# Two PSUM accumulators, deeper rings and bounded row gathers in the edge-gather stage of a GAT + MoE kernel

## What is computed

```python
xp = (x @ W).reshape(N, H, C)                       # N = 3125, H = 4, C = 256
e = leaky_relu(a_src[src] + a_dst[dst], 0.2)        # edges and self loops
ee = jnp.exp(e - m[dst])                            # m: segment max
msgs = xp[src] * (ee / z[dst])[:, :, None]
out = jax.ops.segment_sum(msgs, dst, num_segments=N)   # the stage that is changed
```

## Time and profile before

| | us |
|---|---:|
| median of 3 runs (2448.95 to 2456.05) | 2454.21 |
| the profiled execution | 2455.99 |
| its span, first to last instruction | 2454.2 |

### The profile page before, as it was taken

How to read it: one execution, slowest core, us unless ns; L and a number is a source line. 1 busy time by engine, 2 the same in 40 slices (tenths; PEclk the granted TensorE clock), 3 DMA queues, 4 the chain that set the end, 5 groups by cost and what they waited for, 6 DMA issues and landing times. The chain is left out here.

```text
span 2454.2 us, 53610 instructions
## 1 busy us (share of the span) xinstructions
PE 2006.4 (82%) x14842; PEld 1337.3 (54%) x14843; DVE 1517.5 (62%) x4463; ACT 1115.4 (45%) x2399; POOL 709.3 (29%) x933
## 2 busy tenths in 40 slices
PE   2888897666669999999999387773898999999997
PEld 1455555444438787878888255442344444444553
DVE  3776674777767777777777678877533433433332
ACT  2333432111128787878787355541533433433332
POOL 0002000000016666666665001001222332333332
PEclk9899898555689999999999689995899999999999
DMA  3533344233019999999999455545545546545442
GB/s 131 170 101 112 111 140 138 97 129 123 0 56 353 363 343 362 346 348 354 344 354 333 150 180 184 184 149 189 222 166 215 216 149 216 202 159 168 162 170 80
DMA packets 141057, 489.14 MB, mean 199 GB/s; under 512 B 22449, under 2 KB 22659, under 8 KB 138829
## 3 DMA queue, kind: packets, MB, share of 16 engines
q0 software_dynamic: 98912, 346.99, 40.3%
q1 hardware_dynamic: 41853, 140.70, 15.9%
q10 hardware_dynamic: 216, 0.43, 0.0%
HBM read 418.06 MB, written 81.27 MB: 203 GB/s over the span
## 5 line engine op out<-in xcount | busy, mean ns | idle before, releaser
L1035 PE MATMUL main_ps<-rows,O 128*128 128x256 f16 x4992 | 576.5, 274 | 49.7 <-DVE acc L974 28.6
L1021 ACT ACTIVATE O<-O,pk 128x128 f16<-128x128 f16 x1664 | 499.5, 387 | 126.0 <-DVE O L991 124.3
L1035 PEld LDWEIGHTS main_ps<-rows,O 128*128 128x128 f16 x4992 | 463.7, 98 | 120.1 <-DVE acc L974 33.7
L960 POOL DMA_INDIRECT rows<-projected,idx x416 | 394.6, 948 | 199.5 <-issue 83.7
L1744 PE MATMUL pj_ps<-gram,xsT 128*125 128x512 f16 x1200 | 292.6, 405 | 46.0 <-ACT xsT L396 45.3
L995 DVE TENSOR_SCALAR O<-O,pk 128x128 f16<-128x128 f16 x1664 | 319.2, 270 | 14.9 <-DVE O L991 0.2
L1695 PE MATMUL x_h<-w_p,gram 128*128 x1344 | 309.1, 388 | 17.1 <-ACT gram L1648 11.3
L1710 PE MATMUL x_o<-w_p,gram 128*128 x1344 | 310.8, 382 | 1.4 <-ACT gram L1664 1.4
L1744 PEld LDWEIGHTS pj_ps<-gram,xsT 128*125 128x125 f16 x1200 | 171.0, 146 | 155.8 <-ACT xsT L396 53.5
L1695 PEld LDWEIGHTS x_h<-w_p,gram 128*128 128x128 f16 x1344 | 132.3, 100 | 171.9 <-issue 33.2
L1753 PE MATMUL n_pj<-gram,PK 128*128 128x512 f16 (+3 forms) x900 | 166.5, 344 | 62.1 <-ACT PK L1226 62.1
(11 more groups left out here) (332 smaller groups left out, 2619.2 us busy)
## 6 DMA issues: line engine op xcount, KB each, us to landing
w_f<-in_L_ffn_W_dram SPq DMA_DIRECT2D x14, 2048.0 KB, 12.9
b_t<-in_L_ffn_b_dram SPq DMA_DIRECT2D x56, 512.0 KB, 4.7
xt<-in_x_dram SPq DMA_DIRECT2D x25, 500.0 KB
projected_f<-xp_f POOLq DMA_DIRECT2D x25, 500.0 KB, 3.7
projected<-xp POOLq DMA_DIRECT2D x25, 500.0 KB, 4.8
n_own<-projected_f SPq DMA_DIRECT2D x25, 500.0 KB
n_xt<-in_x_dram SPq DMA_DIRECT2D x25, 500.0 KB
out_dram<-n_x POOLq DMA_DIRECT2D x25, 500.0 KB, 9.9
```

Of the source, the lines that this page charges most:

```text
L960: pool.indirect_dma_start(out=rows[:, 4 * p + k, :, :].rearrange("k n d -> k (n d)"), out_offset=None, in_=xp_d[:, :], in_offset=bass.Indi ...
L1021: ins = act.activation(O[:, k, 1 + HEADS + h, :], O[:, k, 0, :], ACT.Copy, scale=pk[:, p, k, w:w + 1])
L1035: pe.matmul(main_ps[:, h * C:(h + 1) * C], O[:, k, 1 + HEADS * a + h, :], rows[:, 4 * p + k, b, h * C:(h + 1) * C], start=first and h % 2 ...
```

## The change

- `main_ps` and `small_ps` become pairs. A visit uses the member named by the lowest bit of its block number, which each engine takes from the same word (`bank`).
- The one-hots get 8 slots, six in `O` and two in parts of `gram` that nothing else uses.
- The emptying of an accumulator stands six visits behind the building of the one-hots (`LAG`), and the first visit of a block waits for the emptying of the blocks before the last one.
- GpSimd's 416 gathers are written out one by one, read the row numbers directly from `srcT`, and carry a bounds check.
- Row numbers of edges outside a visit's block get 4096 added from visit 8 on, so these rows aren't fetched.

```diff
+RING, LAG, FAR = 8, 6, 4096
+    def bank(u):
+        return ((w >> (BITS * u)) & 1).with_bounds(min_val=0, max_val=1)
+    return block, flag, bank
+
+def of_bank(t, bank):
+    return t[:, bank, :] if isinstance(bank, int) else t[:, bass.ds(bank, 1), :].squeeze(1)
...
+                        off, later = mT[:, RING:VISITS, 0], slice(RING, VISITS)
+                        link(dve.tensor_scalar(off, dlocT[:, later], 0.0, None, ALU.is_lt))
+                        link(dve.scalar_tensor_tensor(off, dlocT[:, later], float(ROWS), off, ALU.is_ge, ALU.add))
+                        link(dve.scalar_tensor_tensor(srcT[:, later], off, float(FAR), srcT[:, later], ALU.mult, ALU.add))
...
-            O = sbuf(c, "O", [P, 4, 1 + 2 * HEADS, P], F16)
+            own_slots = sbuf(c, "O", [P, RING - 2, 1 + 2 * HEADS, P], F16)
+            def O(n, w):
+                if n < RING - 2:
+                    return own_slots[:, n, w, :]
+                i, k = (KD - 1, w) if w < KD - 1 else (KD - 2, w - KD + 1)
+                return gram[:, n - RING + 2, i, k * P:(k + 1) * P]
-            main_ps = psum(c, "main_ps", [P, D])
-            small_ps = psum(c, "small_ps", [P, 512])
+            main_ps = psum(c, "main_ps", [P, 2, D])
+            small_ps = psum(c, "small_ps", [P, 2, 512])
...
                 def _(pool):
-                        if not early(i, 2):
-                            for k in range(4):
-                                wait_apart(pool, s_met, s_row[4 * p + k], 16 * j)
-                        pool.tensor_copy(idx[:, p, :], srcT[:, sl]).then_inc(s_idx, 1)
-                        wait_apart(pool, s_met, s_idx, i + 1)
-                        for k in range(4):
-                            if not early(i, 2):
-                                wait_apart(pool, s_met, s_done, 4 * i - 7 + k)
-                            pool.indirect_dma_start(...)
+                    for v in range(VISITS):
+                        k = v % RING
+                        if v >= RING:
+                            wait_apart(pool, s_met, s_done, v - RING + 1)
+                        pool.indirect_dma_start(
+                            out=rows[:, k, :, :].rearrange("k n d -> k (n d)"), out_offset=None, in_=xp_d[:, :],
+                            in_offset=bass.IndirectOffsetOnAxis(ap=srcT[:, v:v + 1], axis=0),
+                            bounds_check=NODES - 1, oob_is_err=False).then_inc(s_row[k], 16)
...
                 def _(dve):
+                        if not early(i, 2):
+                            wait_apart(dve, s_met, s_lo, 4 * (i - 1))
+                        dve.tensor_copy(pk[:, p, :, :], PK[:, sl, :]).then_inc(s_pk, 1)
+                        if not early(i, 1):
+                            flags = visit_word(dve, words, 1, i - 1)
...
+                            if not early(i, 2):
+                                dve.wait_ge(s_done, v - RING + 1)
+                            dve.tensor_scalar(O(n, 0), iota16[:, :], pk[:, p, k, 0:1], None,
                                               ALU.is_equal).then_inc(s_oh, 1)
...
+                            if k == 1:
+                                if not early(i, 2):
+                                    wait_apart(dve, s_met, s_done, 4 * (i - 1))
+                                dve.tensor_copy(pk16[:, p, :, 0:PACK], PK[:, sl, :]).then_inc(s_hi, 1)
+                            if k % 2 == 1 and not early(v, LAG + 1):
+                                takes((k - 1, k), v - LAG, flags)
...
                 def _(pe):
-                    def products(p, k, first, v=0):
+                    def products(p, k, first, bank, v=0):
+                        n = 4 * p + k
+                        if first and not early(v, 2):
+                            pe.wait_ge(s_seen, 3 * v - 3)
                         for h in range(HEADS):
-                            if first and h % 2 == 0 and not early(v, 1):
-                                pe.wait_ge(s_seen, 3 * v - 2 + h // 2)
                             for a, b in ((0, 0), (0, 1), (1, 0)):
-                                pe.matmul(main_ps[:, h * C:(h + 1) * C], O[:, k, 1 + HEADS * a + h, :],
-                                          rows[:, 4 * p + k, b, h * C:(h + 1) * C],
+                                pe.matmul(of_bank(main_ps, bank)[:, h * C:(h + 1) * C], O(n, 1 + HEADS * a + h),
+                                          rows[:, n, b, h * C:(h + 1) * C],
                                           start=first and h % 2 == 0 and a == b, stop=True, skip_group_check=True)
-                        pe.matmul(small_ps[:, 0:WIDE], O[:, k, 0, :], pk16[:, p, k, 1:1 + WIDE],
+                        pe.matmul(of_bank(small_ps, bank)[:, 0:WIDE], O(n, 0), pk16[:, p, k, 1:1 + WIDE],
                                   start=first, stop=True, skip_group_check=True).then_inc(s_done, 1)
...
-                            pe.wait_ge(s_hi, v + 1)
+                            pe.wait_ge(s_hi, 5 * i + (3, 3, 4, 5)[k])
                             pe.wait_ge(s_lo, v + 1)
...
                             with pe.If(first_at(k) == 1):
-                                products(p, k, True, v)
+                                products(p, k, True, bank_at(k), v)
                             with pe.Else():
-                                products(p, k, False)
+                                products(p, k, False, bank_at(k))
```

More of the change, by code:

```diff
@@ L136, in flag @@
         return (w >> (4 * BITS + u)) & 1
-    return block, flag
+    def bank(u):
[3 more added lines that the diff above has]
+    return t[:, bank, :] if isinstance(bank, int) else t[:, bass.ds(bank, 1), :].squeeze(1)
 class Wider:
@@ L949, in _, with take, takes @@
                 def _(pool):
+                    pool.wait_ge(s_out[0], 32 * (BLOCKS - BLOCKS // 2))
+                    pool.wait_ge(s_out[1], 32 * (BLOCKS // 2))
+                    for v in range(VISITS):
[6 more added lines that the diff above has]
+                            bounds_check=NODES - 1, oob_is_err=False).then_inc(s_row[k], 16)
+                @block.vector
+                def _(dve):
+                    def take(b, bank):
+                        for n in range(2):
+                            half = slice(n * 512, (n + 1) * 512)
+                            a = acc[:, b, half] if isinstance(b, int) else acc[:, bass.ds(b, 1), half].squeeze(1)
+                            dve.tensor_copy(a, of_bank(main_ps, bank)[0:ROWS, half]).then_inc(s_seen, 1)
+                        dve.tensor_copy(at(sacc, b), of_bank(small_ps, bank)[0:ROWS, 0:2 * SUMS]).then_inc(s_seen, 1)
+                    def takes(us, done, flags):
+                        block_at, last_at, bank_at = flags
+                        with dve.If(last_at(us[0]) + last_at(us[1]) > 0):
+                            for n, u in enumerate(us):
+                                wait_apart(dve, s_met, s_done, done + n)
+                                with dve.If(last_at(u) == 1):
+                                    take(block_at(u), bank_at(u))
+                                with dve.Else():
+                                    dve.nop().then_inc(s_seen, 3)
+                        with dve.Else():
+                            dve.nop().then_inc(s_seen, 6)
                     def body(i, j, p):
@@ L957, in body @@
+                        dve.wait_ge(s_pk, i + 1)
                         for k in range(4):
+                            v, n = 4 * i + k, 4 * p + k
                             if not early(i, 2):
[L959 to L962 removed]
```

62 lines of the change are left out of this document (14 added, 48 removed).

## The result

The changed kernel takes **2567.5 us** (median of 4 runs, 2564.31 to 2574.66) against 2451.78 us (4 runs, 2448.95 to 2456.05) on the same chip. The ratio is 1.0476, with an interval of 1.0459 to 1.0493: slower by 4.8%. Its profiled execution took 2566.03 us, with a span of 2564.2.

A forecast was written before the change was run, and what follows sets the result against it. TensorE's matmuls set the pace before, its sequencer after: 415 x 1.70 = 705.5 us against 622.7, +83. With +1 waiting copy, +1 preparation, -1 first gather, +84 gives 2540; the median lies 1.8 lower. Forecast 2538 us, range 2465 to 2605.

The forecast's parts named there:

- The bound: In the gather and product stage, TensorE's sequencer becomes the limit: 1.70 us per visit, 705.5 us against 622.7, +83 us.
- its sum: TensorE's sequencer work before the change: 7.0 us over eight visits, 0.88 per visit, 1.66 at the loop's turn.
- The count: Sequencer instructions added per visit on TensorE: 5 addresses, 1.75 for the bank bit, 0.75 for the s_hi count; 7.5 together.
- The price: Cost of one register instruction on TensorE's sequencer: 0.107 us, with 0.10 and 0.13 as ends; +0.80 us per visit.
- The stalls: TensorE's 24 first-visit waits for emptying the accumulator, 33 to 48 us, removed but not subtracted from the 705.5 us.
- "0" for the rows left out: Not fetching outside edges' rows, 6% of the stage's bytes, gains 0, as TensorE waited for rows only once.
- "0" for the written-out gathers: GpSimd's gathers at 1.31 us per visit instead of 1.455 gain nothing under a 1.70 pace; code fetching taken as 0.
- A: Rival: TensorE's added register work disappears, the stage takes 581 us, 2412 in all; chance 0.13.
- B: Rival: transfers bound the stage at 355 GB/s, so 6% fewer rows give about 2412 us; chance 0.04.
- C: Rival: TensorE's addresses shared or fused to three or four instructions, 1.35 to 1.50 us per visit, 2415 to 2456; chance 0.07.
- D: Rival: address instructions empty the matmul queue or GpSimd stalls on code; over 1.86 us per visit, over 2605; chance 0.04.
- PE's busy time: Sign expected in the profile after: busy PE in the stage stays near 560 to 580 us of some 705.

The follow-up runs named there:

- Experiment 1: Kernel before, with only both accumulators made pairs picked by the register, waits unchanged; ratio to before 1.0174 on one other chip, 1.0167 on a second.
- 3: Changed kernel with the accumulator picked by a second branch with constant addresses; ratio to before 0.9965 and 0.9962 on two other chips.
- 6: Changed kernel with less register work (own semaphore for the pk16 copy, flag tested by mask alone), same addresses; 2550.41 us, ratio to before 0.9984.
- On B: Kernel before, unchanged, on the second of the two other chips used for follow-ups: 2556.3 us; the changed kernel there 2584.04 us.
- experiment 4: Changed kernel with offset 0 in place of 4096, so all rows are fetched; 2580.92 us, ratio to before 1.0084 on the first of two other chips.
- experiment 5: Kernel before with only the new gathers: written out, bounds check, outside rows not fetched; 2565.04 us, ratio to before 1.0045.
- experiment 7: Changed kernel with constant addresses in four arms, less register work and four groups per turn of TensorE's loop; 2786.28 us, ratio to before 1.0902.
- experiment 2: Kernel before with only small_ps made a pair picked by the register, main_ps unchanged; 2567.94 us, ratio to before 1.0039.

## Why the prediction was right

**The bound.** The forecast was 2538 us in a range of 2465 to 2605, and 2567.5 lies in it, 29.5 over the forecast. The step on which all hung was that TensorE's sequencer has 0.88 us of work in a visit that takes 1.353, and that the change adds more than the lead. Experiment 1 adds only that and is slower, 3 and 6 take it away and win back 39 and 34 us. These ran on the other chips; for the first one the size of 115.7 us rests on its own trace, on the count and the price below.

One support of it was luck. The prediction checked its sum on one visit at the loop's turn, 1.66 us against 1.67, and took from it that a visit with more than 1.353 us of sequencer work takes as long as that work and that no queue hides it. Of the 51 turns in that trace 23 took 1.35 to 1.36, the median is 1.47, and only the one shown lies at 1.67. The Trainium skill, Perfetto Trace Analysis, section on the Sequencer Loop, has the sequencer execute control instructions itself and push an engine's instructions into a queue. The trace before agrees: those 23 turns show the sequencer ahead of its matmuls. So single visits are evened out, and what decides is the mean over the turn. In the changed kernel every kind of visit has more than 1.353 us of such work, the lead is gone, and each takes as long as its work: 47 of the 51 turns take 2.45 us or more.

**The count** was exact: 5 + 1.75 + 0.75 predicted, 5.0 + 1.75 + 0.74 seen. One address per place and not per matmul, as read at L1695, holds.

**The price** was the mis-sized term. In the sequencer's visit from 907.02 the five address instructions start 0.124 us apart (907.212, 907.336, 907.460, 907.585, 907.709), plain ALU ones 0.097. The earlier trace rows had given me 0.107 as a mean over both kinds, 0.13 for addresses. The mean of the earlier trace rows is over two ALU instructions for each address, and the change adds twice as many addresses as ALU ones. With the sum's own 0.88 and both measured prices it would have been 0.88 + 5 x 0.124 + 2.5 x 0.097 = 1.74 a visit; I took 1.70; the stage shows 738.2 / 415 = 1.78. So the stage took 738.2 - 705.5 = 32.7 us more than its term, of which the prices explain about half, 0.04 x 415 = 17. The rest, as much again, is not assigned; it can lie in the 0.88, which no row gave directly. The whole missed by less, 2567.5 - 2538 = 29.5, since the later stages took less. The row for the very kind of instruction, was the one to trust over a mean.

**The stalls.** Not subtracting the 33 to 48 us of emptying from the sequencer's bound was right on the first chip: they vanished and nothing came back. On B, before loses more to them (53.7 us in 17 waits of PE, against 28.6 in 24); there the double buffer should be worth more, and together with the cheaper code of 3 it wins 0.4%; the two were not taken apart.

**Gathers and rows.** "0" for the rows left out agrees with experiment 4, as far as ratios from two chips tell. "0" for the written-out gathers was not tested in the changed kernel; in the kernel before on B the whole part cost 9 us (experiment 5). In the changed kernel the gathers follow the products: in the trace after they start 1.56 to 1.85 us apart, one behind a wait for the product:

```profile
902.77 0.98 POOL L975 DMA_INDIRECT rows<-projected,srcT  x1 [0.68 <-issue]
904.33 0.99 POOL L975 DMA_INDIRECT rows<-projected,srcT  x1 [0.57 <-issue]
906.18 0.98 POOL L975 DMA_INDIRECT rows<-projected,srcT  x1 [0.86 <-PE small_ps L1063]
```

**The rivals.** A (registers are free) fell by experiments 1, 3 and 6. B (transfers) needed A and fell with it; that 6% fewer bytes gained nothing in the kernel before (experiment 5) speaks against it too, though on a chip where the stage moves only 299 GB/s. Whether some 355 GB/s would be a limit for a kernel with cheaper sequencer work on the first chip, no run here asked. I had also read the page too simply. A note of the Trainium skill's Perfetto Trace Analysis under Engine Utilization says that 358 GB/s is the share with both cores of a pair active, and that one alone can draw more. The highest slice on any page of the profile here is the 363 of the earlier trace rows. C (half the price) would have needed three or four instructions. D named two ways to be worse, and neither showed on the first chip: the visit is 1.78, under D's 1.86, and the trace after has 49 instruction fetches against 48. Yet the mechanism of D, code that must be fetched, is what experiment 7 ran into on another engine.

**What was wrong among the signs.** I wrote that PE's busy time would stay near 560 to 580 us. It is 635, by the records' tails. And the 1.6 to 1.8 us of an undisturbed visit hold for five of the eight visits of a turn only; the two that load a word take 2.0 and 2.5, and the first behind the word in mid-turn 1.5. The bound of 2577 us for 1.79 a visit is a slip of 2 us (415 x 1.79 gives 2575), which changes nothing.

## What to carry to other kernels

Before a register goes into the address of a matmul, count the sequencer's instructions of one turn at about 0.1 us each (0.10 for an ALU one, 0.12 for an address) and hold them against the time of the turn's matmuls. What exceeds it is paid, in full where nothing else makes TensorE wait; what lies below is nearly free (10 of 122 us in experiment 2). Where it doesn't fit, take the cheap operations away first (a mask in place of shift and mask, counts that several waits share), then put the choice into a branch with constant addresses, as long as the loop's code isn't fetched again: look at the number of instruction fetches on the page after each such step. A double buffer is worth only what the engine behind the stall can then make of it.

## What the runs showed of the hardware

- TensorE's sequencer can be ahead of its matmuls: in the kernel before, 23 of the 51 visits at the loop's turn, with some 1.66 us of sequencer work by the prediction's estimate, passed in 1.35 us, at a mean of 0.88 over the turn.
- On TensorE's sequencer an ALU instruction takes 0.097 us from start to start and an address instruction 0.124, though their durations are 0.036 and 0.046.
- A loop on TensorE with 64 arms of thirteen products each is fetched again in every turn, 275 fetches in the span against 48, and the kernel is 9% slower. Half as many arms, in two different forms, are not (52 fetches each).
- One and the same stage of one and the same kernel took 622.5 us on one chip and 730.9 on another, at equal median durations of its instructions. Beside it the trace of the second shows later signals between engines and a granted clock of 0.96 in place of 1.00. Bound by the sequencer, the changed stage took 738.2 and 749.9. A ratio measured on one chip (1.048) need not be that of another (1.011).
